# POOL's dispatches of token rows without scratch fills and without waits for PE's shared units between them (cross-attention and a mixture of experts, one core)

## What is computed

```python
x = x + xattn(_layernorm(x), ctx_2048, ...)       # latent cross-attention, block by block
xt = _layernorm(x)                                # then the experts
scores = softmax(xt @ Wg.T)                       # 16 experts in 4 groups
# the 2 best groups, in them the 4 best experts of each token
combine = zeros(T, 16).at[token, topi].add(weights)
h = silu(einsum('td,eid->eti', xt, W1)) * einsum('td,eid->eti', xt, W3)
y = einsum('etd,te->td', einsum('eti,edi->etd', h, W2), combine)
z = silu(xt @ Ws1.T) * (xt @ Ws3.T) @ Ws2.T       # shared experts, for every token
x = x + y + z
```

## Time and profile before

| | us |
|---|---|
| median of 3 runs (lowest, highest) | 392.61 (390.57, 393.89) |
| the profiled execution, its own time | 391.41 |
| its span, first to last instruction | 389.4 |
| busy in the span: PE, DVE, ACT, POOL | 321.1, 260.0, 220.4, 198.9 |
| granted TensorE clock, mean | 0.869 of full |

### The profile page before, as it was taken

One profiled execution on the slowest core, in us unless ns is written; L12 is line 12 of the kernel. 1 busy time (PEld: TensorE's weight loads), 2 busy tenths in 40 slices (PEclk: granted clock), 3 DMA queues, 4 the chain that ended last, 5 costly groups with the idle time before them and its releaser, 6 DMA issues.

```text
span 389.4 us, 9334 instructions
## 1 busy us (share of the span) xinstructions
PE 321.1 (82%) x2395; PEld 229.4 (59%) x2396; DVE 260.0 (67%) x982; ACT 220.4 (57%) x553; POOL 198.9 (51%) x239
## 2 busy tenths in 40 slices
PE   0697997977786885357799789999999999996697
PEld 0375665654553554224577557777777777774375
DVE  3457677887787888858855256566666666665764
ACT  0556676655765674244466356666666666653441
POOL 1534333104764675598877015566666666664400
PEclk9998577566968695559999999999999999999599
DMA  8903211222333354332753457887777677779943
GB/s 280 351 1 88 106 64 66 65 66 93 127 129 120 125 156 139 112 141 92 258 188 122 71 100 142 154 168 143 154 159 160 151 150 161 167 220 342 337 142 133
DMA packets 82107, 57.86 MB, mean 149 GB/s; under 512 B 58906, under 2 KB 75549, under 8 KB 82080
## 3 DMA queue, kind: packets, MB, share of 16 engines
q1 hardware_dynamic: 63648, 39.60, 37.7%
q0 software_dynamic: 6912, 17.84, 14.1%
q10 hardware_dynamic: 11520, 0.09, 1.9%
HBM read 24.58 MB, written 24.53 MB: 126 GB/s over the span
## 4 chain that ended last, share of the span: by engine, by line
PE 28%; issue 10%; DVE 8%; POOL 7%; DMA 7%; ACT 2%; SPq 1%; ACTq 1%; POOLq 0%; DVEq 0%
PE bank L741 14%; PE bank L759 9%; POOL ranked L1498 5%; DMA ranked<-ctx_all 5%; PE bank L887 1%; PE bank L747 1%; DMA ctx_all<-slot_rows 1%; POOL slot_rows L1467 1%; DVE hid L1246 1%; PE bank L748 1%; PE bank L749 1%; DVE w L1048 1%; SPq L431 1%; DMA slot_rows<-rows_all,slot_k 1%; ACTq L577 1%
## 5 line engine op out<-in xcount | busy, mean ns | idle before, releaser
L1498 POOL DMA_INDIRECT ranked<-ctx_all x80 | 82.9, 1037 | 69.5 <-issue 35.1
L741 PE MATMUL bank<-w,ctx_all 128*128 x480 | 84.7, 312 | 2.5 <-DMA ctx_all<-slot_rows 2.5
L759 PE MATMUL bank<-w,hT 128*128 (+3 forms) x560 | 80.7, 276 | 2.8 <-ACT ctx_all L592 2.7
L1467 POOL DMA_INDIRECT slot_rows<-rows_all,slot_k x64 | 66.3, 1036 | 15.9 <-issue 14.0
L741 PEld LDWEIGHTS bank<-w,ctx_all 128*128 128x128 f16 x480 | 46.6, 98 | 21.6 <-issue 3.0
L545 ACT ACTIVATE silu<-bank 128x176 f32<-128x176 f32 x112 | 35.4, 316 | 38.0 <-issue 24.4
L1250 DVE TENSOR_TENSOR hh<-hid,hh 128x48 f16<-128x48 f32 x112 | 23.5, 210 | 49.2 <-ACT hh L550 48.7
L550 ACT ACTIVATE hh<-hid 128x176 f16<-128x176 f32 x112 | 39.0, 348 | 29.7 <-DVE hid L1246 26.3
L759 PEld LDWEIGHTS bank<-w,hT 128*128 128x128 f16 (+1 forms) x560 | 50.7, 99 | 7.7 <-issue 3.0
L1246 DVE SCALAR_TENSOR_TENSOR hid<-bank,silu 128x176 f32<-128x176 f32 x112 | 37.4, 334 | 7.9 <-ACT silu L545 7.6
L592 ACT ACTIVATE ctx_all<-bank,ctx_all 128x256 f32<-128x256 f32 x80 | 37.8, 472 | 6.9 <-DMA ranked<-ctx_all 5.5
(11 more groups left out here) (146 smaller groups left out, 563.4 us busy)
## 6 DMA issues: line engine op xcount, KB each, us to landing
wst<-w_dram SPq DMA_DIRECT2D x18, 608.0 KB, 4.0
w<-ranked SPq DMA_DIRECT2D x16, 512.0 KB, 9.5
slot_rows<-pad_rows SPq DMA_DIRECT2D x17, 144.0 KB
x_all<-x_dram SPq DMA_DIRECT2D x4, 512.0 KB, 9.0
ctx_all<-ctx_dram SPq DMA_DIRECT2D x1, 1536.0 KB, 10.5
out_dram<-x_all SPq DMA_DIRECT2D x3, 512.0 KB, 2.9
ctx_all<-slot_rows SPq DMA_TRANSPOSE x80
ctx_all<-slot_rows ACTq DMA_DIRECT2D x80, 1.0 KB
```

What stands on the lines that cost most here:

```text
L741: i = mm(U[j][:, 0:UP1], xt(2 * part + k), up_at(wcol, k, wpart), start=k == 0 and (wpart, part) == (0, 0), stop=k == 1 and wpart == 1)
L759: i = mm(y[:, 0:T], hT[0:rows, j, k * P:(k + 1) * P], down_at(wcol, rows, col), start=start and n == 0, stop=stop and n == len(DOWN) - 1)
L1467: G.indirect_dma_start(scatter_rows, bass.IndirectOffsetOnAxis(ap=slot_k[:, b * TOPK + k:b * TOPK + k + 1], axis=0), rows32[:, b * ROW32:( ...
L1498: G.indirect_dma_start(ranked, bass.IndirectOffsetOnAxis(ap=pair(m)[1], axis=0), y_sb[:, m % YR, :], None, bounds_check=(TOPK + 1) * TOKEN ...
```

## The change

Two things between POOL's dispatches are taken out. The fills: after each dispatch of blocks 8 to 11 POOL waited for its own previous fill and filled a scratch tile of 128x512 with zeros (16 fills). The waits: before each dispatch from block 10, k = 3, on, POOL waited until PE had ended n up projections of the shared units, n from 1 at block 10, k = 3, to 21 at block 15, k = 3 (21 waits). The scratch tile and the semaphore of the fills go with them. The 64 dispatches, their order and the waits for `slot_k`, weights and destinations stay.

```diff
-        PACED = 10
-        SPACED = (8, 12)
-        scratch = sb("scratch", [P, 2 * T])
-        spaced = sem("spaced")
...
             def scatter_to(k):
                 def part(b, u):

-                    n = (b - PACED) * TOPK + k - 2
-                    if n > 0:
-                        pool.wait_ge(SH["up_mm"], min(n, 2 * B1))
                     if u == 0:
                         pool.wait_ge(S["slot_ready"], b + 4)
...
                     G.indirect_dma_start(scatter_rows, bass.IndirectOffsetOnAxis(ap=slot_k[:, b * TOPK + k:b * TOPK + k + 1], axis=0),
                                          rows32[:, b * ROW32:(b + 1) * ROW32], None).then_inc(S["scattered"], 16)
-                    if SPACED[0] <= b < SPACED[1]:
-                        wait(pool, spaced, TOPK * (b - SPACED[0]) + k)
-                        G.memset(scratch[:, :], 0.0).then_inc(spaced, 1)
                 return part
```

## The result

The changed kernel took 389.1 us (median of 20 runs), the kernel before 391.7 (20 runs); the ratio is 0.9943, 95% interval 0.9917 to 0.9968: 2.2 us faster, between 1.3 and 3.3. The forecast was 3.0. Timed again (12 runs) it was 0.9925 (0.9886 to 0.9965). The medians here are of all runs, but every ratio is of those within 1.5% of the same kernel's fastest, which leaves out 3 of 20 here and most where it matters most, 6 of 12 of `c_loads_late` and 5 of 12 of `j_fills_half`: the medians of all their runs are 1.007 and 0.996 of before's.

A forecast was written before the change was run, and what follows sets the result against it. The last dispatch of token rows was taken to decide when expert tiles start. Waits at the tiles 2.5 plus an earlier table 0.5 gave 3.0 us, median from 392.6 to 389.6, range 386.5 to 393.5.

The forecast's parts named there:

- What bounds the start of the expert tiles: Before the expert tiles: the last dispatch, its landing and the first loads decide their start, not PE's own work.
- Where the last dispatch goes: POOL, blocks 8 to 15: without fills and waits the last dispatch starts at 206.4, 6.8 us earlier.
- With the fills gone alone, that wait would still hold it: POOL's last dispatch at 213.18: the wait for the 21st up projection holds it if only the fills go.
- The waits at the tiles: PE at tiles 0 and 2: 1.43 - 0.3 + 1.37 = 2.5 us won, between 1.4 and 2.8.
- The wait for DVE: PE after the down projection of shared unit 23: the 1.59 us wait stays, as DVE's queue stands for that unit.
- The table: End of DVE's routing: expert table 0.5 us earlier as casts are held less; from 0.7 gained to a loss of 1.7.
- The literal reading of the rule: DVE's casts during dispatches: first cast held, second freed, making the sum 2.7 us instead of 3.0.
- `rstd` costs and gains nothing: POOL's `rstd` at 167.70: starting 0.8 us earlier counts nothing; DVE's conversion would release it at the same moment.
- The sign of failure named for the clock: TensorE between 170 and 190: prediction fails if the clock changes at other moments; at 1.2 GHz matmuls take about twice as long.
- (a): PE idle between 217.6 and 230.1: nearly all 4.2 us and 0.7 for casts go, 4.9 us, median 387.7; chance 0.14.
- (b): Expert tiles' start: padding writes or PE address work replace the waits; time stays between 391.5 and 392.6; chance 0.18.
- (c): DVE feeding PE, 172 to 191 us: denser dispatches hold DVE, 3.9 us slower, 396.5; chance 0.18.

The follow-up runs named there:

- c_loads_late: Changed kernel plus a wait in SP's queue before the expert tiles' loads until PE ended all 24 shared up projections; 0.9989 of the kernel before.
- j_fills_half: Changed kernel with the fills of blocks 8 and 9 put back, 8 of 16, no waits for PE; 0.9928 of the kernel before.
- e_add_later: Changed kernel with DVE's addition of shared block 11 moved behind its work on expert tiles 0 and 1; 0.9885 of the kernel before.

## Why the prediction was right, and where not

**What bounds the start of the expert tiles** (last dispatch, landing, loads) was right. The changed kernel, the late loads (0.9989) and the added fills (1.0144) show it from three sides.

**Where the last dispatch goes** without either: 41.8 us after block 8's first, forecast 206.4 - 164.57 = 41.8. The parts of the sum hold too: block 12's first dispatch is 22.9 us after block 8's (189.73), forecast 187.4 - 164.57 = 22.8, and the held dispatch behind DVE's conversion, shifted to the next one, came as forecast (0.98 and 1.32 us; I had let the second be held a little longer).

**"With the fills gone alone, that wait would still hold it"** was wrong in what follows from it. The wait holds, but at a place 2.0 us earlier than the fills did, and there all but 0.4 us of the waits for loads is gone. The step rested on the releaser named in one row; the end of the 21st up projection, 1.9 us before the dispatch, was to be read from PE's timeline. The forecast did not depend on it, since both parts were removed.

**The waits at the tiles.** Tile 0: from 1.43 us to 221.76 - 221.23 = 0.53; I had taken 0.3 for PE's address work, which no row showed alone. Tile 2: 3.06 us behind tile 0 instead of 4.42, 1.36 won, forecast 1.37. The wait for DVE stayed, 1.60 us. Sum 2.3, forecast 2.5.

**The table.** 0.38 us earlier, forecast 0.5. The cast at the end of routing fell from 0.56 to 0.32 us and the integer operation from 0.33 to 0.17, but the 0.30 us of the `slot_k` cast were not on the way to the table: the operations that follow it (L1363, L1246) came at the same place as before. The literal reading of the rule that the prediction gives (first cast held, second free) came out the other way round: the first cast, which began 0.47 us into a dispatch, was free (0.17 us), and the second, 0.61 us into one, was held to its end (0.32). The 2.7 us given for it don't follow from the rows either: with the second cast's 0.40 alone the sum would be 2.9. DVE's timeline after:

```profile
188.94 0.17 DVE L1188 CAST slot_k<-slot_f 128x16 uint32<-128x16 f32 x1
...
190.14 0.17 DVE L1264 TENSOR_SCALAR nt_s<-nt_i 128x16 int32<-128x16 int32 x1
190.35 0.32 DVE L1265 CAST nt_f<-nt_s 128x16 f32<-128x16 int32 x1
```

**`rstd` costs and gains nothing** was right: 1.30 us, held until DVE's conversion ended, its end at the same place. That it is this hold was shown by moving the conversion (0.23 us).

**The sum** was 3.0 us; the landmarks of the trace give 2.3 + 0.4 = 2.6, the timing 2.2 (1.3 to 3.3) and, repeated, 2.9. The median, 389.1, is closer to the forecast 389.6 than the gain is to 3.0, and that is in part luck: before's median of 20 runs is 0.9 us below that of the 3 from which I counted. The sign of failure named for the clock, 1.2 GHz at other moments than before, did come and cost this profile 1.7 us (above), without undoing the gain in the timing.

**The rivals.** (a) More of the start falls away: no, DVE's queue order kept 1.6 us, until it was changed (e_add_later). (b) The wait only exchanged: 0.5 us stay ahead of tile 0, which I take for address work (no run shows what they are), the rest not; beside the padding's writes (DMA engines busy for 0.85) the last 16 dispatches still come every 1.26 us, and tile 0's rows are there before PE is. (c) Dispatches hold DVE: no, the table came earlier, and DVE's small operations during dispatches mostly have their own length.

## What to carry to other kernels

Before costing two delays in a row, find which of them is met last, from the ends of the awaited work and not from the releaser that a row names. A delay ahead of a stage costs nothing until it passes the point where the next stage would wait for it, then one for one; so a delay put in on purpose is worth measuring at half its size. And when a wait falls, read what the first instructions of the next stage stand behind in their own queues: here the order on DVE was worth as much as the change by the landmarks (2.8 and 2.6 us), though only about 1 us of it is in the timing, within its noise.

## What the runs showed of the hardware

A dispatch on POOL locks out DVE's casts and integer operations only in its last part. I read the four such operations at the end of routing (L1192, L1268, L1269 and L1275 in the kernel before) in all 14 profiles, 56 in all. Those that began up to 0.48 us into a dispatch, 19 of them, took 0.17 to 0.19 us, their own length (the 9 that met nothing of POOL took 0.16 to 0.17). Those that began 0.57 to 0.69 us into it, 12 of them, took 0.25 to 0.36 us and all ended 0.02 to 0.03 us before the dispatch's record does. Five that began 0.92 to 1.01 us into longer dispatches (1.13 to 1.22 us) ended at that same place, and two began as a dispatch ended and took 0.16. A fill of zeros holds them to its end: 9 cases in the three kernels with fills there, 0.46 to 0.56 us long, all ending 0.02 to 0.04 us after the fill. The Trainium skill ("SBUF — State Buffer", section "Who interferes with whom") has the second to issue blocked until the first is over. The fills agree; the dispatches, with 0.17 us inside one, do not.

The other way round, DVE's conversion with two SBUF inputs (1.42 us) holds what POOL starts just behind it: an indirect dispatch for 2.22 us instead of 0.97, and an addition on 128x1 for 1.30 instead of 0.23 us. A dispatch that began 0.34 us before the conversion kept its 0.98 us. It doesn't matter how far into the conversion a dispatch begins: in the 14 profiles all 131 dispatches that began during one ended 0.83 to 0.88 us after it.
